# Attention and mixture-of-experts layer: GpSimd norms between pieces of the table scatters, two banks for the last out-projections, one shared unit ahead of the experts

## The chip, the cores and the metric

The kernel runs on one core of one Trainium2 chip. The metric is the device time of one execution in microseconds (us); lower is better. A core has five engines with a queue of instructions each: TensorE (PE, matmuls), VectorE (DVE), ScalarE (ACT), GpSimd (POOL) and SyncE (SP, which here only issues transfers). Each works through its own queue in order, and they hold each other up only by semaphores.

## What is computed

4096 tokens of 512 values pass through one layer: linear attention with decay and an out-projection, a layer norm, a mixture of 64 experts (6 chosen for each token) beside one shared feed-forward network that all tokens take, and a second layer norm.

```python
x = _layernorm(x + attention(x, w_qkv, w_out, decay_param))
scores = softmax(x @ gate_w.T); topk_w, topk_idx = top_k(scores, 6)
# each expert takes its tokens (up to 128) from a table of slots
gx = xp[buf_tok]
g, u = split(einsum('ech,ehi->eci', gx, gate_up_proj))
eo = einsum('eci,eih->ech', silu(g) * u, down_proj) * buf_w[..., None]
routed = zeros.at[buf_tok].add(eo)
shared = silu(xf @ shared_gate_w.T) * (xf @ shared_up_w.T) @ shared_down_w.T
x = _layernorm(x + routed + shared)
```

## The kernel before

The program has three stages. The attention stage runs over 8 blocks of 512 tokens. The tokens are also counted in 32 tiles of 128 (tile i, from 0 to 31; `LAST` is 28 and `HOT` is 27). After attention each tile goes through a chain over all engines: the out-projection on TensorE (`out_rows`, 12 matmuls into a PSUM bank), the sum with the input and its statistics on VectorE (`add_x1`, L1069 to L1034), reciprocal root and shift on GpSimd (`norm`, L1568 to L1572, three tiny instructions), the normed tile on ScalarE (`apply_x1`, L693), its transposition on TensorE (`turn_x1`, L1776), the copy of that on ScalarE (`copy_turned`, L717), the gate matmuls (`gate`), the logits (`copy_logits`, L730 to L737), the choice of six experts on VectorE (`route`), a count of earlier tokens on TensorE (`count_before`, `count_rest`), and the slot of each choice (`place`). For the tiles 0 to 26 the slots go to a table in DRAM by six indirect transfers a tile, which GpSimd issues (`scatter`, L1584). For the tiles 27 to 31 the table is built by one-hot matmuls instead (`place_hot`, `table_add`), and the two are joined (`join_tables`). Then GpSimd gathers each expert's tokens (`gather`, L1615, tile `xg`), 64 experts run, and a last stage makes the final sums.

The routing tail is the stretch in which no attention matmuls are left to cover this chain. TensorE fills it with pieces of the shared network, called units. A unit is 12 matmuls for one third of the gate side (g0, g1, g2) or the up side (u0, u1, u2) of a block of 512 tokens, or 18 matmuls for two tiles of its down side. 8 units of block 0 stand among the last tiles. Units of block 1 follow: `BEFORE_EXPERTS` says how many stand ahead of the last `table_add`, then ahead of the first gathered expert's transposes (`turn_rows(0)`, L1907), and then ahead of `turn_rows(1)`. The rest of blocks 1 to 3 are spread evenly among the experts (`fills_of`), and what is then left stands in the last stage.

All orders are written by hand: each engine's function lists its steps in program order. In the tail GpSimd has the list `scatter(23)`, `norm(27)`, `scatter(24)`, `scatter(25)`, `norm(28)`, `norm(29)`, `scatter(26)`, `norm(30)`, `norm(31)`. TensorE has `out_rows(28)`, `turn_x1(27)`, `out_rows(29)`, `gate(27)`, `out_rows(30)`, `count_before(27)`, `turn_x1(28)`, `out_rows(31)`, and then for i from 28 on `gate(i)`, `turn_x1(i + 1)`, a unit, `count_before(i)`, `table_add(i - 1)`, `count_rest(i)`. ScalarE has for each i `copy_logits(i)`, `copy_turned(i + 1)`, `scale_score(i)`, `apply_x1(i + 2)` and its part of a unit. Every out-projection is written to one bank (`rows_ps`, bank 4), so that `out_rows(i)` waits until VectorE has added tile i - 1.

Of the kernel before, what the change touches and what calls it, by code (L numbers as in the profile page):

```python
# [11 lines left out]
ALU = mybir.AluOpType  # L12
# [5 lines left out]
TOP_K = 6  # L18
# [22 lines left out]
def three(a_hi, a_lo, b_hi, b_lo):  # L41

    return [(a_hi, b_hi), (a_hi, b_lo), (a_lo, b_hi)]


def build(nc, x, x_t, w_qkv, w_out, decay_param, gate_t, w_gu, w_down, sg_t, su_t, sd_t, out):
# [5 lines left out]
    NB = T // BT  # L52
    NJ = BT // P
    NT = T // P
    KC = D // P
# [55 lines left out]
    wout_hi = att.place("wout_hi", [P, KC, D], F32R)  # L111
    wout_lo = att.place("wout_lo", [P, KC, D], F32R)
# [8 lines left out]
    xres = [att.place(f"xres{i}", [P, D]) for i in range(2)]  # L121
# [160 lines left out]
    HOT = LAST - 1  # L282
    AMONG_LAST = 8
    done = AMONG_LAST
    BEFORE_EXPERTS = (1, 3, 1)

    HEAD = 2
    done += sum(BEFORE_EXPERTS)
# [41 lines left out]
    with ExitStack() as ctx:  # L330
# [9 lines left out]
        send_ps = [banks[6], banks[4]]  # L340
        xg_ps, gu_ps, ht_ps, eo_ps = banks[3], banks[4:6], banks[6], banks[7]
        hot_ps = banks[6]


        decay_in, gate_in, table_moved, shared_in = sem("decay_in"), sem("gate_in"), sem("table_moved"), sem("shared_in")
# [654 lines left out]
        def _(dve):  # L1000
# [58 lines left out]
            def add_x1(i):  # L1059
                slot = x1_slot(i)  # L1060
                dve.wait_ge(out_mm, i + 1)
                dve.wait_ge(xres_in[i % 2], 16 * (i // 2 + 1))
                if i >= NJ:
                    dve.wait_ge(turn_mm, i - NJ + 1)
                    dve.wait_ge(x1_out[slot], 16 * (i // NJ))
                    dve.wait_ge(acc_out[slot], 16 * (i // NJ))
                else:
                    dve.wait_ge(stage_lo, NSTAGE)
                dve.tensor_tensor(x1_sb[slot][:, :], rows_ps[:, :], xres[i % 2][:, :], ALU.add).then_inc(x1_added, 1)  # L1069
                dve.wait_ge(x1_added, i + 1)  # L1070
                norm(i, x1_sb[slot][:, :])

# [441 lines left out]
        def _(pool):  # L1514
# [48 lines left out]
            def norm(n):  # L1563
                i = n % len(mv)
                pool.wait_ge(mv_done, n + 1)
                if n >= len(mv):
                    pool.wait_ge(applied, n - len(mv) + 1)
                pool.tensor_scalar(rstd[i][:, :], mv[i][:, 1:2], EPS_NORM, None, ALU.add).then_inc(norm_done, 1)  # L1568
                pool.wait_ge(norm_done, 3 * n + EPS_ADDED)
                pool.tensor_tensor(rstd[i][:, :], rstd[i][:, :], minus_half[:, :], ALU.pow).then_inc(norm_done, 1)  # L1570
                pool.wait_ge(norm_done, 3 * n + ROOTED)
                pool.tensor_scalar(shift[i][:, :], mv[i][:, 0:1], rstd[i][:, 0:1], -1.0, ALU.mult, ALU.mult).then_inc(norm_done, 1)  # L1572
# [3 lines left out]
                if tile:  # L1576
                    norm(tile[0] * NJ + tile[1])

            def scatter(i):
                pool.wait_ge(slot_done, i + 1)  # L1580
                if i == 0:
                    pool.wait_ge(table_moved, TABLE_CLEARED)
                for k in range(TOP_K):
                    pool.indirect_dma_start(  # L1584
                        table_dram, bass.IndirectOffsetOnAxis(slot_of[:, i, k:k + 1], 0), tokens[:, i:i + 1], None,
                        bounds_check=SLOTS - 1, oob_is_err=False).then_inc(scattered, 16)
# [15 lines left out]
            scatter(LAST - 5)  # L1602
            norm(LAST - 1)
            scatter(LAST - 4)
            scatter(LAST - 3)
            norm(LAST)
            norm(LAST + 1)
            scatter(LAST - 2)
            norm(LAST + 2)
            norm(LAST + 3)  # L1610

            def gather(e):
                if e >= NXG:
# [64 lines left out]
        def _(pe):  # L1678
            def chain(out_ap, products, first=True, final=True):
                for i, (a, b) in enumerate(products):  # L1680
                    mm = pe.matmul(out_ap, a, b, start=first and i == 0, stop=final and i == len(products) - 1)  # L1681
                return mm
# [29 lines left out]
            def out_rows(i):  # L1712
                b, j = divmod(i, NJ)
                tok = slice(j * P, (j + 1) * P)
                pe.wait_ge(stage_lo, NSTAGE)
                if i:
                    pe.wait_ge(x1_added, i)

                pe.wait_ge(div_done, KC * (b + 1))
                for k in range(KC):  # L1720
                    pe.wait_ge(att_lo_done, KC * b + k + 1)
                    mm = chain(rows_ps[:, :], three(att_hi[:, k, tok], att_lo[:, k, tok], wout_hi[:, k, :], wout_lo[:, k, :]),
                               first=k == 0, final=k == KC - 1)
                mm.then_inc(out_mm, 1)

# [31 lines left out]
            def table_add(i):  # L1757
                n = i - HOT
                pe.wait_ge(hot_built, n + 1)
                if n == 0:  # L1760
                    pe.wait_ge(div_done, KC * NB)
                parts = [left_low[n % 2]] + ([left_high[n % 2]] if i + 1 < NT else [])
                for k in range(TOP_K):
                    for part in parts:
                        first = n == 0 and k == 0 and part is parts[0]
                        mm = pe.matmul(hot_ps[:, 0:E], slot_is[n % 2][:, k, :], part[:, k, :], start=first, stop=True,
                                       skip_group_check=not first)
                mm.then_inc(hot_mm, 1)
# [219 lines left out]
```

## Time and profile before

| | |
|---|---|
| time of the runs | 921.13 us median of 3 (919.59 to 921.83) |
| the profiled execution's own time | 923.55 us |
| its span in the profile | 921.0 us |
| TensorE busy in the span | 895.2 us, 97% |
| VectorE, ScalarE, GpSimd busy | 719.1, 548.5, 489.6 us |
| TensorE's granted clock, mean | 0.995 of full speed |

The span is what the profile covers; 2.55 us of the execution's own time lie outside it. The busy times of the engines overlap. Times in the rows below are counted from the start of the span.

### The profile page before, as it was taken

What the parts mean: (1) busy time and instruction counts of PE and PEld (TensorE: products, weight loads), DVE (VectorE), ACT (ScalarE), POOL (GpSimd) and SP (SyncE); (2) the same over time, 40 slices, a digit from 0 to 9 for tenths busy, and PEclk for the clock granted to TensorE, in tenths of its full rate; (3) what the DMA queues carried; (4) which work ended last, traced back from release to release, by engine and by line L of the source; (5) the groups of instructions that cost most, each with busy time, mean ns of one, the idle gap of its engine ahead of it and who ended that gap; (6) DMA issues with size and microseconds to landing.
All of it is one profiled execution on the core that took longest, in us unless ns stands there. A gap on an engine that the chain in (4) does not pass through costs nothing. (4 is left out here: it accounts for less than half of the span.)

```text
span 921.0 us, 15578 instructions
## 1 busy us (share of the span) xinstructions
PE 895.2 (97%) x4626; PEld 729.2 (79%) x4626; DVE 719.1 (78%) x1421; ACT 548.5 (60%) x1208; POOL 489.6 (53%) x540
## 2 busy tenths in 40 slices
PE   9999999999999999999899999999999999999996
PEld 7788888888888887777778888888788888777875
DVE  6997888979787887888668777887777887736776
ACT  5532534435353544544458878788877888746784
POOL 2002365565665656587334666665556756433664
PEclk9999999999999999999999999999999999999999
DMA  6343543434262533347468999999999999959973
GB/s 206 99 159 115 157 124 113 129 114 136 84 193 77 161 95 127 110 155 267 161 237 246 324 350 361 352 349 322 325 328 340 353 332 316 295 103 391 380 246 119
DMA packets 116242, 203.95 MB, mean 221 GB/s; under 512 B 18496, under 2 KB 56384, under 8 KB 115136
## 3 DMA queue, kind: packets, MB, share of 16 engines
q1 hardware_dynamic: 95632, 159.87, 50.2%
q0 software_dynamic: 19520, 35.75, 16.3%
q10 hardware_dynamic: 1008, 7.34, 2.0%
q8 instruction: 38, 0.62, 0.3%
q14 instruction: 44, 0.36, 0.1%
HBM read 143.03 MB, written 59.88 MB: 220 GB/s over the span
## 5 line engine op out<-in xcount | busy, mean ns | idle before, releaser
L1584 POOL DMA_INDIRECT slot_table<-tokens,slot_of x162 | 180.5, 1114 | 86.7 <-issue 50.3
L1626 POOL DMA_INDIRECT acc_rows<-eo,table_sb x64 | 140.8, 2199 | 120.4 <-ACT eo L916 57.0
L1681 PE MATMUL bank<-x_hi,wqkv_hi 128*128 128x512 f32 x384 | 152.1, 396 | 0.5 <-DVE wqkv_lo L1007 0.5
L1681 PE MATMUL bank<-x_hi,wqkv_lo 128*128 128x512 f32 x384 | 150.1, 391 | 0.0
L1681 PE MATMUL bank<-x_lo,wqkv_hi 128*128 128x512 f32 x384 | 150.1, 391 | 0.0
L1439 DVE TENSOR_TENSOR wgu_lo<-wgu,wgu_hi 128x1536 fp32r<-128x1536 f32 x64 | 112.0, 1752 | 2.8 <-ACT wgu_hi L902 1.9
L902 ACT CAST wgu_hi<-wgu 128x1536 fp32r<-128x1536 f32 x64 | 94.3, 1474 | 1.6 <-issue 0.4
L1615 POOL DMA_INDIRECT xg<-x_rows,table_sb x64 | 71.6, 1119 | 41.4 <-DVE table_sb L1168 22.1
L1681 PE MATMUL bank<-wgu_hi,xgt_hi 128*128 128x384 f32 x256 | 91.9, 359 | 0.0
L1681 PE MATMUL bank<-wgu_lo,xgt_hi 128*128 128x384 f32 x256 | 86.1, 336 | 0.0
L1681 PE MATMUL bank<-wgu_hi,xgt_lo 128*128 128x384 f32 x256 | 86.0, 336 | 0.0
L672 ACT ACTIVATE e<-bank 128x512 f32<-128x512 f32 x64 | 38.0, 593 | 79.6 <-PE bank L1681 79.6
L1681 PEld LDWEIGHTS bank<-x_hi,wqkv_hi 128*128 128x128 f32 x384 | 72.2, 188 | 16.4 <-issue 1.4
L1681 PEld LDWEIGHTS bank<-x_hi,wqkv_lo 128*128 128x128 f32 x384 | 72.1, 188 | 15.5
L1681 PEld LDWEIGHTS bank<-x_lo,wqkv_hi 128*128 128x128 f32 x384 | 72.2, 188 | 15.1
L1568 POOL TENSOR_SCALAR rstd<-mv 128x1 f32<-128x1 f32 x32 | 9.6, 301 | 124.2 <-DVE mv L1034 122.9
L1681 PE MATMUL bank<-wdn,hid_et 128*128 128x512 f32 x128 | 65.3, 592 | 0.0
L1907 PEld LDWEIGHTS bank<-ident,xg 128*128 128x128 f32 x256 | 30.4, 141 | 35.3 <-issue 25.9
L1452 DVE TENSOR_TENSOR het_lo<-bank,het_hi 128x128 fp32r<-128x128 f32 x64 | 18.6, 290 | 46.0 <-ACT het_hi L955 45.6
L1681 PE MATMUL bank<-wout_hi,att_hi 128*128 128x512 f32 x128 | 52.3, 408 | 1.8 <-issue 1.3
L1681 PE MATMUL bank<-wout_lo,att_hi 128*128 128x512 f32 x128 | 50.2, 392 | 0.0
L1681 PE MATMUL bank<-wout_hi,att_lo 128*128 128x512 f32 x128 | 50.2, 392 | 0.0
(195 smaller groups left out, 2300.2 us busy)
## 6 DMA issues: line engine op xcount, KB each, us to landing
wgu<-w_gu SPq DMA_DIRECT2D x64, 768.0 KB, 7.0
wdn<-w_down SPq DMA_DIRECT2D x64, 384.0 KB, 7.9
xres<-x SPq DMA_DIRECT2D x32, 256.0 KB, 3.2
x_turned<-x1t SPq DMA_DIRECT2D x32, 256.0 KB
x_rows<-x SPq DMA_DIRECT2D x32, 256.0 KB, 3.2
acc_rows<-x SPq DMA_DIRECT2D x32, 256.0 KB, 3.3
fin<-acc_rows SPq DMA_DIRECT2D x8, 1024.0 KB, 12.0
odd<-acc_rows SPq DMA_DIRECT2D x8, 1024.0 KB, 13.9
```

Source lines behind the costliest of these rows:

```text
L672: act.activation(e_sb[q][:, :], ps[:, :], ACT.Exp)
L902: act.copy(wgu_hi[e % 2][:, :, :], wgu_buf[e % NG][:, 0:KS, :]).then_inc(wgu_hi_done, 1)
L1439: dve.tensor_tensor(wgu_lo[e % NG][:, :, :], wgu_buf[e % NG][:, 0:KS, :], wgu_hi[e % 2][:, :, :].bitcast(F32), ALU.subtract).then_inc(wgu_ ...
L1452: dve.tensor_tensor(het_lo[e % 2][:, :], ht_ps[:, P:2 * P], het_hi[e % 2][:, :].bitcast(F32), ALU.subtract).then_inc(het_lo_done, 1)
L1568: pool.tensor_scalar(rstd[i][:, :], mv[i][:, 1:2], EPS_NORM, None, ALU.add).then_inc(norm_done, 1)
L1584: pool.indirect_dma_start(table_dram, bass.IndirectOffsetOnAxis(slot_of[:, i, k:k + 1], 0), tokens[:, i:i + 1], None, bounds_check=SLOTS - ...
L1615: pool.indirect_dma_start(xg[e % NXG][:, :], None, x1_dram, bass.IndirectOffsetOnAxis(table_sb[:, e:e + 1], 0), bounds_check=T - 1, oob_is ...
L1626: pool.indirect_dma_start(acc_dram[e % 2], bass.IndirectOffsetOnAxis(table_sb[:, e:e + 1], 0), eo[eo_slot[e]][:, :], None, bounds_check=T ...
L1681: mm = pe.matmul(out_ap, a, b, start=first and i == 0, stop=final and i == len(products) - 1)
L1907: mm = pe.transpose(xg_ps[:, k * P:(k + 1) * P], xg[e % NXG][:, k * P:(k + 1) * P], ident[:, :])
```

## The change

GpSimd's last norms no longer wait for whole scatters: the 12 scatter transfers behind which `norm(28)` stood, and the six behind which `norm(30)` stood, are cut into pieces of three and two with a norm after each. The out-projections of tiles 29 and 31 go to bank 6, those of 28 and 30 stay in bank 4, and each waits only for the sum before the last. The one-hot table, which also lives in bank 6, now starts after the last sum. One unit more stands ahead of `turn_rows(0)`, and with it one less among the experts.

```diff
-    BEFORE_EXPERTS = (1, 3, 1)
+    BEFORE_EXPERTS = (1, 4, 1)
...
+        def rows_bank(i):
+            return banks[6] if i >= LAST and i % 2 else rows_ps
...
-                dve.tensor_tensor(x1_sb[slot][:, :], rows_ps[:, :], xres[i % 2][:, :], ALU.add).then_inc(x1_added, 1)
+                dve.tensor_tensor(x1_sb[slot][:, :], rows_bank(i)[:, :], xres[i % 2][:, :], ALU.add).then_inc(x1_added, 1)
...
-            def scatter(i):
+            def scatter(i, ranks=range(TOP_K)):
...
-                for k in range(TOP_K):
+                for k in ranks:
...
             scatter(LAST - 4)
-            scatter(LAST - 3)
+            scatter(LAST - 3, range(3))
             norm(LAST)
+            scatter(LAST - 3, range(3, TOP_K))
             norm(LAST + 1)
-            scatter(LAST - 2)
+            scatter(LAST - 2, range(2))
             norm(LAST + 2)
+            scatter(LAST - 2, range(2, 4))
             norm(LAST + 3)
+            scatter(LAST - 2, range(4, TOP_K))
...
-                    pe.wait_ge(x1_added, i)
+                    pe.wait_ge(x1_added, i - 1 if i > LAST else i)
...
-                    mm = chain(rows_ps[:, :], three(att_hi[:, k, tok], att_lo[:, k, tok], wout_hi[:, k, :], wout_lo[:, k, :]),
+                    mm = chain(rows_bank(i)[:, :], three(att_hi[:, k, tok], att_lo[:, k, tok], wout_hi[:, k, :], wout_lo[:, k, :]),
...
                 if n == 0:
-                    pe.wait_ge(div_done, KC * NB)
+                    pe.wait_ge(x1_added, NT)
```

On GpSimd the last scatters and norms stood in this order before; `rstd_57` to `rstd_60` are the four buffers, which serve tiles 28 to 31 here.

```order
L1584 DMA slot_table<-tokens,slot_of 8192x1 x12
L1568 TENSOR_SCALAR rstd_57<-mv_53 128x1
L1570 TENSOR_TENSOR rstd_57<-rstd_57,minus_half 128x1
L1572 TENSOR_SCALAR shift_61<-mv_53,rstd_57 128x1
L1568 TENSOR_SCALAR rstd_58<-mv_54 128x1
L1570 TENSOR_TENSOR rstd_58<-rstd_58,minus_half 128x1
L1572 TENSOR_SCALAR shift_62<-mv_54,rstd_58 128x1
L1584 DMA slot_table<-tokens,slot_of 8192x1 x6
L1568 TENSOR_SCALAR rstd_59<-mv_55 128x1
L1570 TENSOR_TENSOR rstd_59<-rstd_59,minus_half 128x1
L1572 TENSOR_SCALAR shift_63<-mv_55,rstd_59 128x1
```

The same place on GpSimd now, from the first piece on:

```order
L1587 DMA slot_table<-tokens,slot_of 8192x1 x9
L1571 TENSOR_SCALAR rstd_57<-mv_53 128x1
L1573 TENSOR_TENSOR rstd_57<-rstd_57,minus_half 128x1
L1575 TENSOR_SCALAR shift_61<-mv_53,rstd_57 128x1
L1587 DMA slot_table<-tokens,slot_of 8192x1 x3
L1571 TENSOR_SCALAR rstd_58<-mv_54 128x1
L1573 TENSOR_TENSOR rstd_58<-rstd_58,minus_half 128x1
L1575 TENSOR_SCALAR shift_62<-mv_54,rstd_58 128x1
L1587 DMA slot_table<-tokens,slot_of 8192x1 x2
L1571 TENSOR_SCALAR rstd_59<-mv_55 128x1
L1573 TENSOR_TENSOR rstd_59<-rstd_59,minus_half 128x1
L1575 TENSOR_SCALAR shift_63<-mv_55,rstd_59 128x1
```

`norm(28)` moved ahead of three of its twelve transfers, and `norm(30)` ahead of four of its six; `norm(29)` has three transfers directly ahead of it where it had none.

On TensorE, where the third expert-side unit ended and the first gathered expert is transposed (`xg0`), the order before was this; `su` belongs to an up unit, `sg` to a gate unit, and the brackets name the semaphores.

```order
L1681 MATMUL bank1<-x1t_hi_170,su_hi_159 128x512
L1681 MATMUL bank1<-x1t_lo_163,su_hi_159 128x512
L1681 MATMUL bank1<-x1t_hi_170,su_lo_160 128x512
L1907 MATMUL bank3<-ident_49,xg0_183 128x128 [waits score_done,xg_in0,table_done,x1t_done]
L1907 MATMUL bank3<-ident_49,xg0_183 128x128 x3
L1681 MATMUL bank2<-x1t_hi_170,sg_hi_164 128x512 [waits hid_s_done,x1t_lo_done,shared_split]
L1681 MATMUL bank2<-x1t_lo_163,sg_hi_164 128x512
L1681 MATMUL bank2<-x1t_hi_170,sg_lo_161 128x512
```

On TensorE at that place now:

```order
L1687 MATMUL bank2<-x1t_hi_170,sg_hi_164 128x512
L1687 MATMUL bank2<-x1t_lo_163,sg_hi_164 128x512
L1687 MATMUL bank2<-x1t_hi_170,sg_lo_161 128x512
L1913 MATMUL bank3<-ident_49,xg0_183 128x128 [waits score_done,xg_in0,table_done,x1t_done]
L1913 MATMUL bank3<-ident_49,xg0_183 128x128 x3
L1687 MATMUL bank0<-x1t_hi_170,su_hi_159 128x512 [waits silu_done,x1t_lo_done,shared_split]
L1687 MATMUL bank0<-x1t_lo_163,su_hi_159 128x512
L1687 MATMUL bank0<-x1t_hi_170,su_lo_160 128x512
```

The gate unit g2 of block 1 moved from behind `turn_rows(0)` to ahead of it, and u2 took its old place.

## Rows read from the trace of the kernel before

**Rows 1.** The page, part 1, TensorE's row.
```profile
PE 895.2 (97%) x4626; PEld 729.2 (79%) x4626; DVE 719.1 (78%) x1421; ACT 548.5 (60%) x1208; POOL 489.6 (53%) x540
```

**Rows 2.** TensorE's timeline, start, length, engine, line, [idle before].
```profile
426.53 0.47 PE L1681 MATMUL bank<-wout_hi,att_hi 128*128 128x512 f32 x1 [0.76 <-issue]
...
429.37 1.00 PE L1681 MATMUL bank<-gate_sb,x1t 128*128 128x64 f32 x8
...
434.41 0.66 PE L1776 MATMUL bank<-ident,x 128*128 128x128 f32 x4 [1.00 <-ACT x L693]
...
438.62 0.61 PE L1776 MATMUL bank<-ident,x 128*128 128x128 f32 x4
...
441.84 0.20 PE L1749 MATMUL bank<-any_choice,before 128*128 128x64 bf16 x1
...
446.33 0.74 PE L1776 MATMUL bank<-ident,x 128*128 128x128 f32 x4 [2.79 <-ACT x L693]
...
451.16 0.20 PE L1749 MATMUL bank<-any_choice,before 128*128 128x64 bf16 x1
...
476.73 0.63 PE L1907 MATMUL bank<-ident,xg 128*128 128x128 f32 x4 [1.10 <-DMA xg<-x_rows,table_sb]
```

**Rows 3.** GpSimd's timeline among the last scatters and norms.
```profile
426.31 0.97 POOL L1584 DMA_INDIRECT slot_table<-tokens,slot_of  x1 [0.30 <-issue]
...
435.25 1.09 POOL L1584 DMA_INDIRECT slot_table<-tokens,slot_of  x1 [0.43 <-issue]
436.65 1.71 POOL L1584 DMA_INDIRECT slot_table<-tokens,slot_of  x1 [0.30 <-issue]
...
443.51 0.34 POOL L1568 TENSOR_SCALAR rstd<-mv 128x1 f32<-128x1 f32 x1
...
445.16 0.27 POOL L1572 TENSOR_SCALAR shift<-mv,rstd 128x1 f32<-128x1 f32 x1
445.51 0.22 POOL L1568 TENSOR_SCALAR rstd<-mv 128x1 f32<-128x1 f32 x1
...
446.48 0.27 POOL L1572 TENSOR_SCALAR shift<-mv,rstd 128x1 f32<-128x1 f32 x1
```

**Rows 4.** Line 1584, the table scatters, over the whole span.
```profile
L1584 POOL DMA_INDIRECT slot_table<-tokens,slot_of x162: 962/972/2369, 103.2 to 442.5; - x162
```

**Rows 5.** ScalarE's timeline in the tail.
```profile
428.62 0.58 ACT L717 COPY x1t<-bank 128x512 f32<-128x512 f32 x1
...
433.54 0.81 ACT L693 ACTIVATE x<-x,shift,rstd 128x512 f32<-128x512 f32 x1 [1.47 <-POOL shift L1572]
...
441.08 0.35 ACT L707 ACTIVATE score<-e_route,r_sum 128x64 f32<-128x64 f32 x1
445.46 0.81 ACT L693 ACTIVATE x<-x,shift,rstd 128x512 f32<-128x512 f32 x1 [4.03 <-POOL shift L1572]
```

**Rows 6.** VectorE's timeline: tile 28's statistics, the one-hot build, the table.
```profile
427.19 0.18 DVE L1034 BATCH_NORM_AGGREGATE mv<-stats 128x2 f32<-128x6 f32 x1
...
443.68 0.95 DVE L1156 TENSOR_TENSOR slot_is<-slot_no,position 128x768 bf16<-128x768 f32 x1
...
463.63 0.17 DVE L1161 CAST table_f<-table_sb 128x64 f32<-128x64 uint32 x1
```

**Rows 7.** Windows: busy of each engine, granted clock, DMA share, GB/s.
```profile
448.00:450.00 2.00, 2.00 (x6) 1.52 (x6) 0.46 (x3) 1.75 (x5) 0.00 (x0) 0.50 0.04 10
```

**Rows 8.** SyncE's queue: the load of the finished table.
```profile
457.88 0.43 SPq L592 DMA_DIRECT2D table_sb<-slot_table  x1
```

**Rows 9.** GpSimd's waits, 480 to 820 us.
```profile
POOL acc_rows L1626 <- ACT eo L916: 57.0, 19, 13.6
POOL acc_rows L1626 <- DMA acc_rows<-eo,table_sb: 50.9, 26, 4.2
```

**Rows 10.** Tile xg, the gathers: time from issue to landing.
```profile
DMA to landing us min/median/max: 4.2/7.7/12.0
```

**Rows 11.** TensorE's timeline among the experts, the longest gather wait.
```profile
668.58 1.09 PE L1907 MATMUL bank<-ident,xg 128*128 128x128 f32 x4 [1.99 <-DMA xg<-x_rows,table_sb]
```

## The prediction

> **What bounds the kernel now.** I read the page first: TensorE is busy for 895.2 of 921.0 us [rows 1]. So time can only come from TensorE's idle stretches and from matmuls that ran slowly, and everything else matters only through them. The second view is TensorE's timeline in the stretch of the change [rows 2], where the reader is to see four gaps: 0.76 us before the out-projection of tile 29 (426.53), 1.00 us before the transposes of tile 28 (434.41), 2.79 us before those of tile 30 (446.33), and 1.10 us before those of the first gathered expert (476.73). The third view is GpSimd's timeline. ScalarE's normed tile is late because GpSimd's norm is: the norm of tile 30 starts at 443.51, directly behind six scatters, and ends at 445.43 [rows 3]; a scatter takes 0.97 us in the median [rows 4] and the next starts 0.30 us later, a period of 1.27 us. ScalarE had been free for that tile since 441.43 (441.08 + 0.35), and started at 445.46 [rows 5].
>
> **Two banks.** The out-projection of tile 29 no longer waits for VectorE's sum of tile 28, so it starts up to 0.76 us sooner. Next in TensorE's queue is gate(27), though, which needs the transposed copy of tile 27: ScalarE ends it at 429.20 [rows 5], against gate(27)'s start at 429.37 [rows 2]. With the 0.06 us that such a handover takes (434.35, the end of ScalarE's tile 28 in [rows 5], to 434.41), gate(27) starts at 429.26. The banks alone give 0.11 us; the rest of the gap moves behind tile 29's matmuls.
>
> **The norm of tile 28.** The third scatter of tile 25 ends at 427.28 (426.31 + 0.97 [rows 3]), and VectorE's aggregate of tile 28 at 427.37 [rows 6], so the norm starts near 427.45. A norm takes 1.24 us (445.51 to 446.75) or 1.92 us (443.51 to 445.43) [rows 3], so it ends at 428.7 to 429.4. ScalarE was idle for 1.47 us before its tile 28, so it could start at 432.07 [rows 5], which is later than the norm in either case; the tile is ready at 432.88. TensorE was free for the transposes at 433.41 (434.41 less its idle 1.00), or 433.30 after the 0.11 us. So the whole 1.00 us goes. TensorE is 1.11 us ahead.
>
> **The norms of tiles 30 and 31.** After the norm of 28 come three scatters, norm 29, two scatters, norm 30. From a norm to the next scatter I take 0.43 us (the gap in brackets ahead of 435.25 [rows 3] is that between norm 29 and the scatter), from a scatter to a norm 0.08 us, as between two norms (445.43 to 445.51). Three scatters take 3 x 1.27 - 0.30 = 3.51 us, two take 2.24 us; with a slow one (1.71 instead of 0.97 us [rows 3]) add 0.74. Fast: norm 29 ends at 428.7 + 0.43 + 3.51 + 0.08 + 1.24 = 434.0, norm 30 at 434.0 + 0.43 + 2.24 + 0.08 + 1.24 = 438.0. With every norm at 1.92 and one slow scatter in each piece: 436.1 and 441.5. ScalarE gets to tile 30 at 441.43 - 1.11 = 440.3 and needs 0.81 us [rows 5]: the tile is ready at 441.1, or 442.3 in the slow case. TensorE would be free for its transposes at 446.33 - 2.79 - 1.11 = 442.43 [rows 2]. Both are in time, so the whole 2.79 us goes. Norm 31, one piece and one norm later, ends at 442.0 or 446.9, its tile at 442.8 or 447.7. TensorE wants it behind a count and a gate of 1.00 us, before at 452.2 or later (451.16 + 1.00 [rows 2]), now 5.5 us sooner with the clock's part below, so at 446.7: the slow case costs up to 1.0 us. I take the fast one, since only one norm in the rows stood under such VectorE work.
>
> Rows and a rule differ on which norm length to expect. In the rows the 1.92 us norm (443.51) lies under VectorE's `slot_is` (443.68, 0.95 us, both inputs in SBUF), and the 1.24 us norm under no such work [rows 3, 6]. The Trainium skill, page GPSIMD Engine Reference, section Specifications, says that GpSimd's way to SBUF is shared with VectorE and that instructions with two SBUF inputs contend. By it the norms, now put among VectorE's busiest routing work, would all be slow, which is the slow case above; the trace agrees with it at that one place. The sum would be 5.6 us by the rule and is 6.6 us by the short norms.
>
> **The clock.** After the 2.79 us gap the granted clock reads 0.50, the 1.2 GHz level, from 448 to 450 us [rows 7]. The transposes of tile 30 with their unit and count took 446.33 to 451.16, 4.83 us; the same work for tile 29 took 438.62 to 441.84, 3.22 us [rows 2]. Without the gap the second figure should hold: 1.61 us more. TensorE had idled 1.00 us ahead of 434.41 and the unit from 438.62 still came at full pace, so a short gap that remains at 428.4 (0.8 us) costs no clock.
>
> **The unit moved.** TensorE waited 1.10 us for the first gather at 476.73, and this wait sits behind the last `table_add`, from where everything (table, gathers, loads) moves with TensorE. A unit takes up to 3.22 us, more than 1.10, so it covers the wait. On ScalarE its activation now stands ahead of the copy of the first gathered tokens; even at 0.81 us, the longest pass over a tile in [rows 5], that delay lies under unit u2, which TensorE does next. No step of SyncE's queue moves. It is not work added, since the experts have one unit less. Gain 1.10 us, if the experts stay bound by TensorE. The ends of this cost: at most 1.10, at least 0 if the gathers come later by as much as the unit.
>
> **Sum.** 0.11 + 1.00 + 2.79 + 1.61 + 1.10 = 6.6 us. The profiled execution's own 923.55 us would become 916.9; it stood 2.4 us above the median of the runs shown. Taken off the median of 921.13 us the forecast is 914.5 us.
>
> **Rivals.** (A) the sum holds, 914.5, range 913.2 to 916; chance 0.56.
>
> (B) The experts don't give the moved unit back. They run close to GpSimd's pace too: between 480 and 820 us it waited 50.9 us for the sum transfers before the last to land, and 57.0 us for ScalarE's results, which is its whole reserve [rows 9]; gathers stand behind these sums in its queue, and land after 4.2 to 12.0 us [rows 10]. Where transfers set the pace, a unit less buys nothing: the gain is 6.6 - 3.2 = 3.4, 917.7 us. For it: TensorE once waited 1.99 us for a gather (668.58), and its four transposes then took 1.09 us [rows 11]. Against it: the reserve of 57 us over 64 experts. Chance 0.15.
>
> (C) The clock still falls at another moment, or a norm is later than worked out, and 1.6 us stay lost: 916.1. Chance 0.11.
>
> (D) More than the sum: the same shifts also remove the gather wait among the experts, 1.99 us and about as much again in slow matmuls, as 1.61 followed 2.79 above: 3.6 more, 910.9. The position of gathers against sums is all that decides it. Chance 0.10.
>
> (E) The table comes late. The last scatters are now issued behind four norms instead of ahead of two, up to 450.3 us (446.9 + 0.43 + two scatters with a slow one, 2.98) instead of 443.4. The table's load waits for them on SyncE (457.88 [rows 8], 452.4 after the shift) and VectorE reads the table at 463.63 [rows 6], 458.1 after it. How long a scatter takes to land no row shows; it is at most 14.4 us, from 443.5 to 457.88, and more than nothing. With 2.3 us for the load (0.43 for its issue, the rest my allowance, well inside the 5.75 us from 457.88 to 463.63), scatters that land within 5.5 us cost nothing even when all is slow. The nearest rows are the gathers' 4.2 to 12.0 us, of far larger transfers at full load; I take the low end. At 12.0 the cost would be 6.5 (921.0, no change); at 14.4 it is 8.9, 2.3 us slower than before, 923.4. Chance 0.04, all of it within 0.3%. By the Trainium skill, page DMA: Bandwidth & Descriptors, section Anatomy of one DMA, such a small transfer takes about 2.0 us, an estimate by which this rival costs nothing; no row here shows it.
>
> (F) Slower: TensorE, with a unit less among the experts, catches up with the gathers and stops for them as in [rows 11], each time at 3.6 us. Two more such stops than before leave no measurable change (6.6 - 7.2 = -0.6, 921.7); three end at 925.3. It decides from the second stop on. For and against it stands what is said under (B). Chance 0.02 for two, 0.02 for three or more.
>
> **How the numbers follow.** What a measurement can tell from no change is 0.3%, 2.8 us: faster is below 918.4, slower above 923.9. A to D are faster: 0.92. Same is E and the first half of F, 0.06; slower 0.02. The range runs from between A and D (911.9) to just past B (918.2). That leaves out most of D and all of E and F, some 0.17.
>
> **What would show it.** In the changed profile: norms of 28, 30 and 31 that start at about 427.5, 436.7 to 439.6 and 440.7 to 445 us; transposes of tile 30 near 442.4 with no wait; the granted clock at 1.00 through 440 to 458; about 0.8 us idle ahead of gate(27); no wait before the first expert's transposes, which start near 473 us (476.73 - 1.10 - 5.5 + one unit); the last expert 6.6 us sooner. The prediction is wrong if a wait for ScalarE's tile 30 or 31 stays, if a wait on the table appears near 458, or if the gain at the first expert shrinks until the last.

## The result and the profile after

The changed kernel took 914.85 us in the median of 8 runs (912.43 to 917.59), the kernel before beside it 920.99 us (919.05 to 923.27, 8 runs). The ratio is 0.9935, with a 95% interval of 0.9918 to 0.9951: 6.1 us faster, against a forecast of 914.5 us. The profiled execution took 912.62 us, with a span of 910.9 us, so it is one of the faster ones. The four faster of the eight runs (912.4 to 914.3) have a mean granted clock of 0.997 to 0.999, the four slower (915.4 to 917.6) all 0.996. That matters below. Here and in the experiments the ratios leave out three executions on record that took far longer than all others: 994 us of the kernel before on the second chip, 1799 us of `e5_split5` and 4623 us of `e4_no_unit`.

In the changed kernel the lines of TensorE's instructions stand 6 further down than before, those of the other engines 3. First the page's busy times, which answer to [rows 1].

```profile
PE 891.4 (98%) x4626; PEld 726.2 (80%) x4626; DVE 719.0 (79%) x1421; ACT 548.3 (60%) x1208; POOL 486.2 (53%) x540
```

The number of matmuls is unchanged and their busy time is 3.8 us shorter: in this pair of profiles, that is the part of the gain which is not waiting but pace. TensorE's timeline in the tail answers to [rows 2] (start, length, engine, line, idle before):

```profile
429.36 1.10 PE L1687 MATMUL bank<-gate_sb,x1t 128*128 128x64 f32 x8 [0.72 <-ACT x1t L720]
...
433.17 0.64 PE L1782 MATMUL bank<-ident,x 128*128 128x128 f32 x4
...
437.36 0.61 PE L1782 MATMUL bank<-ident,x 128*128 128x128 f32 x4
...
442.10 0.61 PE L1782 MATMUL bank<-ident,x 128*128 128x128 f32 x4
...
445.30 0.20 PE L1755 MATMUL bank<-any_choice,before 128*128 128x64 bf16 x1
...
472.32 0.60 PE L1913 MATMUL bank<-ident,xg 128*128 128x128 f32 x4
```

Three brackets of [rows 2] are gone: the transposes of tile 28 (433.17), of tile 30 (442.10) and of the first expert (472.32) start without a wait. One gap has moved: the 0.76 us ahead of out-projection 29 is now 0.72 us ahead of gate(27), at 429.36. A gap that moves to the next instruction is how a removed wait looks when a second one stands close behind it.

The whole stretch in one window (busy of PE, PEld, DVE, ACT, POOL, then granted clock, DMA share, GB/s):

```profile
440.00:458.00 18.00, 17.76 (x136) 14.22 (x135) 14.88 (x53) 10.44 (x31) 4.97 (x7) 1.00 0.52 170
```

The granted clock is 1.00, the 2.4 GHz level, throughout; in [rows 7] it was 0.50 for two of these microseconds. GpSimd's timeline answers to [rows 3]:

```profile
427.58 0.23 POOL L1571 TENSOR_SCALAR rstd<-mv 128x1 f32<-128x1 f32 x1 [0.18 <-DVE mv L1037]
...
428.56 0.27 POOL L1575 TENSOR_SCALAR shift<-mv,rstd 128x1 f32<-128x1 f32 x1
...
433.12 0.37 POOL L1571 TENSOR_SCALAR rstd<-mv 128x1 f32<-128x1 f32 x1
...
437.36 0.23 POOL L1571 TENSOR_SCALAR rstd<-mv 128x1 f32<-128x1 f32 x1
...
438.35 0.27 POOL L1575 TENSOR_SCALAR shift<-mv,rstd 128x1 f32<-128x1 f32 x1
...
441.46 0.62 POOL L1571 TENSOR_SCALAR rstd<-mv 128x1 f32<-128x1 f32 x1
442.17 0.58 POOL L1573 TENSOR_TENSOR rstd<-rstd,minus_half 128x1 f32<-128x1 f32 x1
442.85 0.64 POOL L1575 TENSOR_SCALAR shift<-mv,rstd 128x1 f32<-128x1 f32 x1
...
445.04 0.97 POOL L1587 DMA_INDIRECT slot_table<-tokens,slot_of  x1 [0.30 <-issue]
```

Norm 30 starts at 437.36 where it started at 443.51, and ends at 438.62. Norm 28 takes 1.25 us (427.58 to 428.83) and norm 30 1.26 us; norm 31 takes 2.03 us (441.46 to 443.49). VectorE's timeline shows what lies over norm 31, and when the table is read:

```profile
441.40 0.56 DVE L1146 TENSOR_TENSOR expert_is<-before_end,nearest 128x384 bf16<-128x384 f32 x1
...
442.40 0.95 DVE L1159 TENSOR_TENSOR slot_is<-slot_no,position 128x768 bf16<-128x768 f32 x1
...
457.77 0.17 DVE L1164 CAST table_f<-table_sb 128x64 f32<-128x64 uint32 x1
```

Norm 31 lies under `expert_is` and `slot_is`, two operations with two inputs each. The Trainium skill, page GPSIMD Engine Reference, section Specifications, says that such instructions contend with GpSimd for the way to SBUF. This trace agrees: norm 31 is the slow one of the four, 2.03 us against 1.25 to 1.40. Its middle operation (442.17) took the usual 0.58 us all the same, though `slot_is` ran from 442.40 on. ScalarE's normed tiles, which answer to [rows 5], show that even the slow norm was in time:

```profile
431.87 0.80 ACT L696 ACTIVATE x<-x,shift,rstd 128x512 f32<-128x512 f32 x1
...
440.87 0.80 ACT L696 ACTIVATE x<-x,shift,rstd 128x512 f32<-128x512 f32 x1
...
445.42 0.80 ACT L696 ACTIVATE x<-x,shift,rstd 128x512 f32<-128x512 f32 x1
```

None has idle time ahead of it that a norm ended, and the last starts 1.9 us after norm 31 is done.

The table is loaded by SyncE at 452.02, and the last scatter's issue ended at 446.01 (445.04 + 0.97):

```profile
452.02 0.43 SPq L595 DMA_DIRECT2D table_sb<-slot_table  x1
```

Among the experts TensorE stops three times for a gather, and the last expert's down-projection starts at 805.90:

```profile
523.16 0.66 PE L1913 MATMUL bank<-ident,xg 128*128 128x128 f32 x4 [0.93 <-DMA xg<-x_rows,table_sb]
...
656.06 0.66 PE L1913 MATMUL bank<-ident,xg 128*128 128x128 f32 x4 [0.55 <-DMA xg<-x_rows,table_sb]
...
785.18 0.66 PE L1913 MATMUL bank<-ident,xg 128*128 128x128 f32 x4 [0.79 <-DMA xg<-x_rows,table_sb]
...
805.90 0.50 PE L1687 MATMUL bank<-wdn_mix,het_hi 128*128 128x512 f32 x1 [1.21 <-DVE het_lo L1455]
```

The kernel before, in the same view, stops twice: at 668.58 for 1.99 us [rows 11] and once more for 1.17 us; and it reaches the same down-projection at 816.29:

```profile
795.57 0.66 PE L1907 MATMUL bank<-ident,xg 128*128 128x128 f32 x4 [1.17 <-DMA xg<-x_rows,table_sb]
...
816.29 0.50 PE L1681 MATMUL bank<-wdn_mix,het_hi 128*128 128x512 f32 x1 [1.21 <-DVE het_lo L1452]
```

So in this pair of profiles the changed kernel is 5.86 us ahead at the count in the tail (445.30 against 451.16), 10.39 us ahead at the last expert, and 10.1 us at the end of the span, while the medians differ by 6.1 us. The forecast's own sign, the last expert 6.6 us sooner, does not show in this pair. The experiments below had to tell which part belongs to the change.

### The profile page after: what moved, and what is told of

It is laid out like the page before. It is cut to its first block and busy times, and to the rows that moved or that the text cites. A ratio compares the mean times of both kernels' runs of the same rounds, so it can differ in the third digit from the quotient of the medians.

```text
span 910.9 us, 15578 instructions
## 1 busy us (share of the span) xinstructions
PE 891.4 (98%) x4626; PEld 726.2 (80%) x4626; DVE 719.0 (79%) x1421; ACT 548.3 (60%) x1208; POOL 486.2 (53%) x540
## 5 line engine op out<-in xcount | busy, mean ns | idle before, releaser
L1632 POOL DMA_INDIRECT acc_rows<-eo,table_sb x64 | 135.5, 2117 | 118.5 <-DMA acc_rows<-eo,table_sb 64.0
L1621 POOL DMA_INDIRECT xg<-x_rows,table_sb x64 | 74.3, 1161 | 36.2 <-issue 18.7
```

Of the source, the lines that this page charges most:

```text
L1621: pool.indirect_dma_start(xg[e % NXG][:, :], None, x1_dram, bass.IndirectOffsetOnAxis(table_sb[:, e:e + 1], 0), bounds_check=T - 1, oob_is ...
L1632: pool.indirect_dma_start(acc_dram[e % 2], bass.IndirectOffsetOnAxis(table_sb[:, e:e + 1], 0), eo[eo_slot[e]][:, :], None, bounds_check=T ...
```

## Experiments

Each kernel was timed in five rounds beside the kernel before on the same chip. Four chips served. On the first, the kernel before took 920.62 us in the median (23 runs), like the 920.99 above. On the others it took 927.5 to 928.9 us. Only ratios are compared across chips. The changed kernel itself was timed only for the result above, so a comparison with its 0.9935 is always one between two ratios.

### The three edits alone, and two of them together (second chip, kernel before 928.06 us)

Of the diff shown above, `e1_norms_only` has the parts on `scatter` and the list of norms, `e2_banks_only` those on `rows_bank`, `x1_added` and the one-hot table's start, `e3_unit_only` has only this line, and `e4_no_unit` everything but it:

```diff
-    BEFORE_EXPERTS = (1, 3, 1)
+    BEFORE_EXPERTS = (1, 4, 1)
```

> The kernel before, with only GpSimd's norms placed between pieces of the scatters; one bank and three units ahead of the first gathered expert as before. Theory 1 (the norms carry the gain): the waits of 1.00 and 2.79 us go and the granted clock stays at 1.00, 5.4 us in all, ratio 0.994; the 0.76 us wait for the bank and the 1.10 us wait for the first gather stay. Theory 2 (the tail's gain is given back among the experts, and the measured gain came from fewer gather stops there): the first expert starts 5.4 us sooner but the last one hardly does, ratio 0.998 or more.

> The kernel before, with only the second bank for the out-projections of tiles 29 and 31. Theory 1: the 0.76 us wait turns into a wait of gate(27) for ScalarE's transposed copy, the stretch to the transposes of tile 28 gains 0.1 us at most, and nothing changes after the 2.79 us wait for tile 30: ratio 1.000. A rival in which the bank mattered by itself: 0.7 us, 0.999, with the transposes of tile 30 as much sooner.

> The kernel before, with only the fourth unit ahead of the first gathered expert. Theory 1: the 1.10 us wait at 476.7 goes, everything before it is unchanged, ratio 0.999; the last expert ends 1.1 us sooner. Rival (transfers set the pace of the experts): the first expert starts 1.7 us later and the last one ends later than before or more gather waits appear, ratio 1.001 or more.

> The changed kernel with three units again ahead of the first gathered expert, so norms and banks without the unit. Theory 1: 5.5 us less than before, ratio 0.994, 1.1 us more than the changed kernel, and a wait of about 1.1 us before the first gathered expert's transposes near 470.8. Rival: no wait there, because the gathers land sooner against TensorE than before.

| kernel | median us | ratio to before | 95% interval |
|---|---|---|---|
| norms only | 921.50 | 0.9945 | 0.9928 to 0.9963 |
| banks only | 926.32 | 0.9997 | 0.9981 to 1.0014 |
| unit only | 926.71 | 0.9993 | 0.9975 to 1.0012 |
| norms and banks | 921.30 | 0.9943 | 0.9922 to 0.9963 |

The norms carry nearly all of it. The other two can't be told from nothing, which is what 0.1 and 1.1 us are beside an interval of about 1.6 us to either side. The gains of the three alone add to 0.65%, and the whole change gave 0.65% on a chip like the first. The unit's mechanism shows in the profiles: with three units TensorE waited 0.53 to 1.42 us ahead of the first expert in all seven profiles of such kernels (0.53 us with norms and banks, where 1.1 was expected), and with four or more in none of seven.

The place, however, is not the same on this chip. In the profile of banks only, which still has the old list of norms, the idle time of TensorE stands elsewhere: here its timeline, and then VectorE's.

```profile
434.22 0.23 PE L1757 MATMUL bank<-any_choice,not_before 128*128 128x64 bf16 x1 [4.45 <-DVE before_end L1180]
...
482.72 0.63 PE L1910 MATMUL bank<-ident,xg 128*128 128x128 f32 x4 [0.77 <-DMA xg<-x_rows,table_sb]
```

```profile
433.94 0.22 DVE L1180 TENSOR_TENSOR before_end<-any_choice,bank 128x64 f32<-128x64 bf16 x1 [4.06 <-remote]
```

VectorE idled 4.06 us ahead of `before_end`, although the count that it reads had been done since 425.4; the profile puts this down to "remote", to no engine and no transfer of the kernel. TensorE waited behind it, and no wait for a normed tile shows. In the profile of norms only the first gathered expert starts at 476.57, 6.15 us sooner than here, but that is the fastest of its eleven runs, and the new list of norms does not rule such a wait out: in `e9_unit7`, on the third chip, TensorE idles 3.79 us at the same place (435.72). So the medians confirm the size of the gain on the second chip. Where it arises there, and whether through the wait for tile 30, is not shown. The next group is from the first chip, whose traces have no such wait.

### How much of the scatter has to go behind the norm (first chip)

The kernel before, with `norm(30)` and `norm(31)` ahead of the last one (`e5_split5`) or the last two (`e6_split4`) of the six transfers, and nothing else changed. Shown for the second:

```diff
             norm(LAST)
             norm(LAST + 1)
-            scatter(LAST - 2)
+            scatter(LAST - 2, range(4))
             norm(LAST + 2)
             norm(LAST + 3)
+            scatter(LAST - 2, range(4, TOP_K))
```

> The kernel before, with the norms of tiles 30 and 31 placed ahead of the last one of the six scatters of tile 26, nothing else. TensorE's wait for tile 30 should shrink from 2.79 to about 1.5 us (one scatter period of 1.27 less). If the lost matmul speed hangs on the wait's length, two outcomes: the granted clock stays at 1.00 and the gain is 1.3 + 1.6 = 2.9 us (ratio 0.997), or it still falls to 0.5 and the gain is 1.3 us (0.9986). The waits seen so far leave it open: 1.17 us did not cost speed, 1.99 us did.

> The kernel before, with those two norms placed ahead of the last two scatters of tile 26. The wait for tile 30 should be 0 to 0.3 us, the clock 1.00 and the gain 4.2 us (ratio 0.9954), the greater part of what the whole change brings. A rival in which the clock falls for another reason than this wait: 2.7 us (0.997) and a granted clock below 1.00 around 448 us.

Measured: 917.38 us, ratio 0.9973 (0.9958 to 0.9987) with one transfer behind, and 916.19 us, 0.9955 (0.9937 to 0.9973) with two. TensorE's timeline and the windows of the first, where tile 30's transposes start at 444.78:

```profile
444.78 0.66 PE L1777 MATMUL bank<-ident,x 128*128 128x128 f32 x4 [0.87 <-ACT x L693]
```

```profile
446.00:448.00 2.00, 2.00 (x10) 1.48 (x8) 0.81 (x6) 1.87 (x6) 1.09 (x1) 1.00 0.04 8
448.00:450.00 2.00, 2.00 (x28) 1.89 (x27) 1.66 (x8) 0.20 (x1) 0.00 (x0) 1.00 0.68 233
```

And of the second, whose second row is a wait among its experts:

```profile
442.84 0.61 PE L1777 MATMUL bank<-ident,x 128*128 128x128 f32 x4
...
663.69 0.66 PE L1908 MATMUL bank<-ident,xg 128*128 128x128 f32 x4 [1.78 <-DMA xg<-x_rows,table_sb]
```

One transfer less ahead of the norm takes 1.92 us off the wait of 2.79 us [rows 2] and leaves 0.87; a second takes the rest. The expectation was a wait of 1.5 us, one period of 1.27 us less. The other 0.65 us come from the norm's length, as GpSimd's timeline of the first shows:

```profile
443.61 0.27 POOL L1572 TENSOR_SCALAR shift<-mv,rstd 128x1 f32<-128x1 f32 x1
443.95 0.28 POOL L1568 TENSOR_SCALAR rstd<-mv 128x1 f32<-128x1 f32 x1
444.31 1.13 POOL L1570 TENSOR_TENSOR rstd<-rstd,minus_half 128x1 f32<-128x1 f32 x1
```

Norm 30, moved forward, takes 1.25 us (442.63 to 443.88) where it took 1.92, and norm 31 now takes the long operation of 1.13 us in its place, under VectorE's `slot_is` (444.07 to 445.01).

With 0.87 us left the granted clock reads 1.00 where it read 0.50 in [rows 7]. This is the experiment that shows the clock's share of the gain: by this profile beside that of the kernel before the gain is 1.92 us of waiting and 1.6 us of pace, 3.5 us; the medians differ by 3.2 us, while the ratio gives 2.5 us with an interval of 1.2 to 3.9. That interval also holds the 1.92 us of waiting alone, so the clock's share rests on the windows and not on the times.

### Does the table come late? (first chip)

The changed kernel, with the last four transfers all behind `norm(31)`:

```diff
             scatter(LAST - 2, range(2))
             norm(LAST + 2)
-            scatter(LAST - 2, range(2, 4))
             norm(LAST + 3)
-            scatter(LAST - 2, range(4, TOP_K))
+            scatter(LAST - 2, range(2, TOP_K))
```

> The changed kernel, with the last four scatters of tile 26 all behind the norm of tile 31, so that the last one is issued about 1.3 us later against the norms and none stands between the norms of 30 and 31. If scatters land within some 4 us (theory 1), the table's load is not delayed and the time is that of the changed kernel within 0.3 us. If they take as long as the gathers (rival E of the prediction, 8 to 12 us), VectorE waits for the table near 458 us and the kernel is 1 to 3 us slower than the changed one.

Measured: 914.55 us, ratio 0.9936 (0.9916 to 0.9956), no different from the changed kernel. GpSimd's timeline, and then SyncE's:

```profile
445.42 0.97 POOL L1587 DMA_INDIRECT slot_table<-tokens,slot_of  x1 [0.30 <-issue]
```

```profile
452.72 0.43 SPq L595 DMA_DIRECT2D table_sb<-slot_table  x1
```

The last transfer's issue ends at 446.39, hardly later than in the changed kernel: what stands behind the norm instead of ahead of it moves no end. The run thus puts no more strain on the table than the changed kernel does, and tests rival E no further. The table's load, which waits for all scatters, comes 6.3 us after, and 6.0 us after in the changed kernel, so a scatter has landed within 6.0 us. How much less it takes was not tried.

### One more edit in the tail: the copy of tile 27 first (first chip)

The changed kernel, with ScalarE's copy of tile 27's transposed rows ahead of its part of a unit, against the 0.72 us that gate(27) waits:

```diff
             apply_x1(LAST - 1)
-            unit()
             copy_turned(LAST - 1)
+            unit()
```

> The changed kernel, with ScalarE's transposed copy of tile 27 ahead of its part of the unit instead of behind it. The 0.72 us wait of gate(27), into which the wait for the bank had turned, should go: TensorE 0.7 us sooner at the transposes of tile 28 and after, ratio to before 0.0008 lower than the changed kernel's 0.9935. If ScalarE's hid_hi is what the chain needs next, VectorE's hid_lo comes 0.6 us later and part of it is lost again.

Measured: 911.98 us (910.91 to 915.08), ratio 0.9908 (0.9891 to 0.9925). TensorE's timeline:

```profile
427.88 1.00 PE L1687 MATMUL bank<-gate_sb,x1t 128*128 128x64 f32 x8
...
432.12 0.66 PE L1782 MATMUL bank<-ident,x 128*128 128x128 f32 x4 [0.37 <-ACT x L696]
...
471.54 0.60 PE L1913 MATMUL bank<-ident,xg 128*128 128x128 f32 x4
```

The wait of 0.72 us is gone; 0.37 us of it stands again ahead of the transposes of tile 28. The first expert starts 0.78 us sooner than in the changed kernel (472.32). The spans differ by 1.2 us, the ratios by 0.27%, 2.5 us, where 0.7 us was expected, and their intervals overlap. The tail shows 0.8 us of it; where the rest comes from, if it is more than noise, is not shown.

### Do the experts give a moved unit back, and the gathers (third chip, kernel before 928.89 us)

`e9_unit7` is the changed kernel with three more units ahead of the first expert; `e10_ahead5` is the changed kernel with each expert's tokens gathered five experts ahead where four were.

```diff
-    BEFORE_EXPERTS = (1, 4, 1)
+    BEFORE_EXPERTS = (1, 7, 1)
```

```diff
-    NG, ND, NXG, AHEAD = 5, 5, 6, 4
+    NG, ND, NXG, AHEAD = 5, 5, 6, 5
```

> The changed kernel with seven units instead of four between the last table_add and the first gathered expert's transposes, so four fewer among the experts than in the kernel before, not one. Theory 1 (the experts are bound by TensorE): a unit costs the same wherever it stands, the last expert ends within 1 us of the changed kernel's, ratio as the changed kernel's, 0.9935. Rival B of the prediction (the gathers and sums set the experts' pace when units are fewer): each unit moved away loses part of its 2.75 us, more and longer waits for gathers, 3 to 8 us slower than the changed kernel (0.997 to 1.002).

> The changed kernel with the gathers issued five experts ahead instead of four. If TensorE's stops among the experts (0.5 to 2.0 us, two or three a run) are gathers that land late, they go: 2 to 3 us less than the changed kernel, ratio 0.991, and the runs spread less. The price could be GpSimd waiting for an expert's result before the gather and so issuing the next sum later; then the waits for gathers stay or grow and the ratio is 0.994 or more.

Measured: 925.68 us, ratio 0.9939 (0.9915 to 0.9963) with the units, and 923.49 us, 0.9915 (0.9881 to 0.9949) with the gathers. The kernel before falls into two groups on this chip, ten runs from 927.3 to 930.5 us and seven from 933.0 to 936.3, and the ratios weigh both; beside the first group alone they would be 0.997 and 0.995. So the time does not settle rival B: 0.9939 is theory 1's, and 0.997 is where the rival's range starts. The traces do. TensorE from the first gathered expert's transposes to the last expert's down-projection, first in the kernel before, then in the changed kernel, then with three more units moved out of this stretch:

```profile
476.73:816.29 339.56, 333.56 (x1705) 276.18 (x1705) 262.88 (x475) 269.29 (x550) 202.59 (x121) 0.99 0.98 317
```

```profile
472.32:805.90 333.58, 328.95 (x1693) 272.05 (x1691) 262.06 (x474) 268.91 (x549) 199.06 (x120) 1.00 0.98 321
```

```profile
495.14:818.91 323.77, 318.81 (x1645) 262.61 (x1643) 257.12 (x468) 264.27 (x541) 194.45 (x120) 1.00 0.99 329
```

The stretch is 9.8 us shorter with three units (48 matmuls) less, and TensorE idles 5.0 us in it where it idled 4.6. The experts give the moved units back but for some 0.3 us, where rival B would have asked about 3 us for each.

With the gathers one further ahead TensorE has no wait for `xg` left. The gain of this over the changed kernel lies inside the intervals; `e12_before_ahead5` below is the run that shows it. GpSimd's waits from 480 to 820 us, first the changed kernel's, then this one's (us in total, times, longest):

```profile
POOL acc_rows L1632 <- DMA acc_rows<-eo,table_sb: 64.0, 33, 3.2
POOL acc_rows L1632 <- ACT eo L919: 46.8, 14, 16.0
```

```profile
POOL xg L1621 <- ACT eo L919: 39.3, 13, 16.0
POOL acc_rows L1632 <- DMA acc_rows<-eo,table_sb: 31.6, 17, 3.0
POOL acc_rows L1632 <- ACT eo L919: 25.6, 14, 3.0
```

The waits of a sum for the last sum's transfer fall from 64.0 to 31.6 us, and GpSimd now waits for ScalarE ahead of the gathers too: of 111 us of such waits 97 are left, part of them at another place.

### Both extras, and the gathers alone (fourth chip, kernel before 927.51 us)

`e11_both` is the changed kernel with the edits of the last two sections, `e12_before_ahead5` the kernel before with the gathers' edit alone.

> The changed kernel with both extras at once: ScalarE copies tile 27's transposed rows ahead of its part of a unit, and each expert's tokens are gathered five experts ahead where four were. Alone the first made the changed kernel's median 2.6 us lower on the same chip, and the second left no wait for a gather among the experts (ratio 0.9915 to the kernel before). Theory 1: the first acts in the tail, the second among the experts, so both add: 0.5 us more than the changed kernel's sum in the tail, about 2 us (one or two gather waits with their slow matmuls) among the experts; ratio about 0.990, the profile without a wait for xg and with gate(27) straight behind tile 29's out-projection. Rival: the copy's 2.6 us were themselves a luckier position of the gathers, so with the gathers out of the way the copy adds only its 0.5 us; ratio 0.991, no better than either alone.

> The kernel before with the gathers five experts ahead where four were, and nothing else. It leaves the tail as it was, so the 2.79 us wait for tile 30 with its slow matmuls and the 1.10 us wait for the first gather stay. Theory 1: the two later waits for gathers (1.99 and about 1.2 us, the longer with slow matmuls) go, 3 to 4 us in a profile that has them both, about 2 us in the median; ratio 0.9975. Rival: the experts give a wait for a gather back elsewhere, in a wait for a buffer or in the last stage; ratio 1.000.

Measured: 915.63 us, ratio 0.9880 (0.9857 to 0.9904), and 925.12 us, 0.9971 (0.9949 to 0.9993). No wait for a gather among the experts is left in either; the second idles 0.72 us ahead of the first one (481.44). The 2.79 us wait for tile 30, which the expectation of the second took over from the first chip, is not in its profile: TensorE idles 1.54 and 3.05 us (427.18 and 430.43) before it comes to that place. The extras add: 0.92% with the copy and 0.29% with the gathers make 1.21%, and both together gave 1.20%. The rival of `e11_both`, 0.991, lies outside its interval, though by less than 0.1%. This is the best kernel of the study, 11.9 us below the kernel before on its chip, nearly twice the gain of the change.

## Why the prediction was right, point by point

**Two banks, 0.11 us.** As forecast: gate(27) starts at 429.36, 0.01 us sooner than in [rows 2], in a profile whose TensorE came to this stretch 0.1 us later (transposes of tile 27 at 425.23 against 425.12), and the wait ahead of it, forecast as 0.8 us, is 0.72. Alone the banks are not to be told from no change.

**The norm of tile 28, 1.00 us.** The norm started at 427.58 (forecast 427.45) and was a short one. The transposes came 1.24 us sooner (433.17 against 434.41), where 1.11 was the sum so far.

**The norms of tiles 30 and 31, 2.79 us.** Norm 30 started at 437.36 and ended at 438.62, within the forecast's ends of 438.0 and 441.5. The transposes started at 442.10 with no wait; the forecast was 442.43. Norm 31 was slow, as the rule had it, and still ended 1.9 us ahead of ScalarE's pass, so the 1.0 us put down for the slow case was not paid. The choice of the fast sum was right in its size, but the ground given for it was half right: three of four norms met no two-input work for long, the fourth did. The reading behind it, that only one norm before stood under such work, was wrong. Norm 28 was slow too, 1.88 us, with VectorE's `sd_lo` (432.18 to 433.45) over its last operation:

```profile
432.61 0.90 POOL L1572 TENSOR_SCALAR shift<-mv,rstd 128x1 f32<-128x1 f32 x1
```

**The clock, 1.61 us.** The count came at 445.30, 5.86 us sooner than in [rows 2], and the transposes 4.23 us sooner: 1.63 us of pace. That the clock comes back when the wait shrinks, not only when it goes, is shown by `e5_split5`.

**The unit, 1.10 us.** The wait is gone at 472.32 (forecast: near 473), on the fourth unit. The unit's edit alone has an interval that holds both 1.1 us and nothing, and so does the step from norms and banks (0.9943) to the whole (0.9935). The trace shows the mechanism; the time does not resolve it.

**The sum, 6.6 us against 6.1 measured.** The terms ahead of the experts came out at 6.96 us in the pair of profiles (5.86 and 1.10). Read at the first expert it is 7.2: 4.41 us sooner (472.32 against 476.73) with a unit more, some 2.8 us of matmuls, already done.

**The rivals.** B falls by the traces: three more units moved left the experts' idle time within 0.4 us of what it was. Its price was too high besides: the 3.2 us hold the transposes as well, and a unit's own matmuls take 2.8 us. C did not happen. E did not happen: the last scatter was issued at 445.04, not at up to 450.3, and landed within 6.0 us. F did not happen: three stops for gathers stand where there were two, but the longest is 0.93 us and none took pace with it. D happened in the profiled execution. From the first to the last expert it is 5.98 us shorter than the profile before (333.58 against 339.56): 2.8 us are the unit that moved, 1.4 us are less idle time, of it 0.9 us for gathers (2.3 against 3.2) and 0.4 us for `het_lo` (1.2 against 1.6), and the remaining 1.8 us are pace. The pace fits the matmuls behind the 1.99 us stop, whose granted clock averages 0.72 over 668 to 674, and 0.28 of 6 us is 1.7. But whether an execution has a long gather stop changes from run to run and from kernel to kernel. `e6_split4` had a stop of 1.78 us, and `e7_late_scatters`, whose median is the changed kernel's, two with 3.4 us in all; none of these took pace with it. So the position of gathers against sums is not fixed by the change. That the median carries the sum without D is the likely reading. The granted clocks of the eight runs fit it: they are 0.998 in the mean of the four faster and 0.996 in the slower, which over 911 us makes some 2 us of the 3.6 us between the two halves. But only one of these runs was profiled, so it is argued and not shown.

## What to carry to other kernels

Where an engine issues many transfers in a row, ask which tiny computation stands behind them in its queue: here 1.9 us of GpSimd's work behind six issues of some 1.3 us each held TensorE, and two transfers moved behind it gave two thirds of the whole gain. Price a wait on TensorE with the pace of the matmuls after it, read from the window behind it; it need not shrink in proportion, and here all of it was there at 2.79 us of waiting and none at 0.87. And when the profile of one execution gains more than the medians, look for waits that come and go by themselves before crediting the change.

## What the runs showed of the hardware

**How long a wait costs pace.** The same two readings, idle time ahead of a TensorE instruction and the granted clock just after it, stand in many of these traces. Full pace followed waits of 0.87, 1.00, 1.17, 1.34, 1.42, 1.52, 1.78 and 1.89 us. The clock fell to 0.50, the 1.2 GHz level, after 1.99 us [rows 11] and 2.79 us [rows 7]. A window of that stop of 1.99 us, in the kernel before:

```profile
670.00:672.00 2.00, 2.00 (x8) 2.00 (x8) 1.39 (x2) 1.61 (x5) 0.00 (x0) 0.50 1.03 406
```

It also fell after waits of 2.32 us (norms and banks, second chip) and, one just behind the other, of 2.03 and 1.42 us (gathers five ahead, third chip). The latter's window:

```profile
434.00:436.00 2.00, 2.00 (x6) 1.62 (x5) 1.32 (x4) 0.89 (x3) 0.00 (x0) 0.50 0.08 17
```

But the length alone does not decide it. In `e12_before_ahead5` a single wait of 1.41 us was enough:

```profile
412.05 0.20 PE L1749 MATMUL bank<-any_choice,before 128*128 128x64 bf16 x1 [1.41 <-issue]
```

```profile
414.00:416.00 2.00, 2.00 (x6) 1.63 (x5) 0.62 (x3) 0.80 (x2) 1.30 (x4) 0.50 0.97 309
```

At the same count five other traces have waits of 1.39 to 1.43 us (411.18 to 411.97), and full pace behind them. In `e3_unit_only` the clock fell within 2 us of a wait of 1.48 us (434.07), with one of 0.99 us behind it. So from 1.4 us on the traces show both outcomes, up to the 1.89 us that still kept full pace. What else decides it these rows don't say: the waits have different work around them.

**A chip can have waits of its own.** The kernel before takes 921 us on the first chip and 928 on the three others. In the traces of those three TensorE idles for more in the stretch from 395 to 450 us, often at the same places (1.4 us ahead of a count near 411.7, for one, in all four traces of the second chip), and the other engines' waits there are put down to "remote", up to 4.1 us each on VectorE. The kernel has no partner off the core. What they are stays open.

**GpSimd's norms** take 1.25 us alone and 1.9 to 2.0 us under VectorE's two-input work. In these traces an operation of a norm that began while such an instruction ran ended only behind it: 442.85 to 443.49 with `slot_is` until 443.35, and 432.61 to 433.51 with `sd_lo` until 433.45 in the kernel before. One that began first was not lengthened: 0.58 us from 442.17, with `slot_is` from 442.40. The lengths grow from 0.23 to 0.62, from 0.57 to 1.13 and from 0.27 to 0.90 us at most. No run takes the VectorE work away, so this is read from where they overlap. The issue of an indirect transfer, 0.97 us in the quiet, took 1.24 us behind norm 28.
